# A quarter of the second layer's row maxima taken from half sums and half differences of the keys

## The reference, cut to what matters

```
x_n = (x - mu) * rsqrt(var + eps) * ln_gamma + ln_beta
q, k, v = split(x_n @ W_qkv + b_qkv)                 # 16 heads of 8
scores = einsum('bhqd,bhkd->bhqk', q, k) * SCALE
scores = scores - max(scores, axis=-1)
attn = exp(scores); attn = attn / max(sum(attn), 1e-12)
out = einsum('bhqk,bhkd->bhqd', attn, v) @ W_proj + b_proj
```

## Time and profile before

| what | value |
|---|---|
| median of 3 runs | 3652.12 us (3650.84 to 3652.28) |
| the profiled execution, its own time | 3654.05 us |
| its span in the trace | 3652.2 us |
| TensorE busy | 2988.8 us (82%) |
| VectorE busy | 2628.4 us (72%) |
| ScalarE busy | 2149.4 us (59%) |
| second layer's projection, first store to the end | 909.75 to 958.54 us |
| second layer's attention | 958.54 to about 1672 us |

### The profile page before, as it was taken

One profiled execution on the slowest core, in us unless ns is written; L12 is line 12 of the kernel. 1 busy time (PEld: TensorE's weight loads), 2 busy tenths in 40 slices (PEclk: granted clock), 3 DMA queues, 4 the chain that ended last, 5 costly groups with the idle time before them and its releaser, 6 DMA issues. The chain is left out here.

```text
span 3652.2 us, 51682 instructions
## 1 busy us (share of the span) xinstructions
PE 2988.8 (82%) x18320; PEld 1208.1 (33%) x18320; DVE 2628.4 (72%) x6022; ACT 2149.4 (59%) x2736; POOL 454.0 (12%) x601
## 2 busy tenths in 40 slices
PE   2599998897699999996599999976369998989836
PEld 1133333343222222223355555554332222222214
DVE  4699995476699999984566666641678888888831
ACT  2166666222277777784355545542269989989822
POOL 2000000333100000000000000003231010102023
PEclk9699999998699999998699999987779999999968
DMA  5532220422531211200000000011263222221102
GB/s 201 154 54 46 49 42 2 94 47 54 181 50 35 39 32 30 31 1 4 30 1 1 1 7 1 7 52 43 78 147 55 33 31 30 28 36 23 52 15 81
DMA packets 168110, 173.42 MB, mean 47 GB/s; under 512 B 46648, under 2 KB 126280, under 8 KB 165296
## 3 DMA queue, kind: packets, MB, share of 16 engines
q1 hardware_dynamic: 163760, 162.38, 20.8%
q0 software_dynamic: 4096, 7.78, 0.7%
HBM read 107.71 MB, written 62.26 MB: 47 GB/s over the span
## 5 line engine op out<-in xcount | busy, mean ns | idle before, releaser
L1194 ACT ACTIVATE a_probs<-a_scores 128x1024 f32<-128x1024 f32 (+3 forms) x896 | 791.3, 932 | 374.9 <-PE a_scores L1091 234.2
L1217 DVE TENSOR_REDUCE a_part_max<-a_slot_ps 128x1 f32<-128x512 f32 x1280 | 798.0, 682 | 42.2 <-PE a_slot_ps L1069 40.6
L1069 PE MATMUL a_slot_ps<-a_k_op,a_q_op 48*128 48x512 bf16 (+3 forms) x1792 | 579.7, 380 | 123.1 <-DMA a_mask_wide<-in_mask_wide 32.4
L2214 DVE TENSOR_TENSOR a_probs<-a_logit_ps,a_gate 128x1024 f32<-128x1024 f32 x512 | 602.0, 1218 | 98.0 <-ACT a_gate L2073 96.4
L2078 ACT ACTIVATE a_probs<-a_probs 128x2048 f32<-128x2048 f32 x256 | 488.0, 1906 | 8.6 <-DVE a_probs L2214 8.6
L1091 PE MATMUL a_scores<-a_q_op,a_k_op 51*128 51x512 bf16 (+3 forms) x1792 | 453.2, 362 | 7.1 <-ACT a_probs L1194 6.1
L1111 PE MATMUL a_o_ps<-a_probs,a_v_op 128*32 128x512 f32 (+3 forms) x3584 | 438.1, 561 | 1.2 <-ACT a_o_sb L1181 0.6
L1069 PEld LDWEIGHTS a_slot_ps<-a_k_op,a_q_op 48*128 48x128 bf16 x1792 | 150.3, 94 | 725.0 <-DVE a_part_max L1217 468.2
L1979 PE MATMUL a_logit_ps<-space 96*128 96x512 bf16 x1024 | 303.0, 387 | 72.4 <-DVE a_probs L2214 64.0
L2073 ACT ACTIVATE a_gate<-a_diff_ps 128x1024 f32<-128x1024 f32 x256 | 261.3, 1021 | 54.9 <-PE a_diff_ps L1979 47.3
L1992 PE MATMUL a_o_ps<-a_probs,a_v_op 128*32 128x512 f32 x2048 | 274.6, 608 | 7.0 <-DVE a_o_sb L2207 3.1
(11 more groups left out here) (389 smaller groups left out, 3777.0 us busy)
## 6 DMA issues: line engine op xcount, KB each, us to landing
scratch_v<-p_vpad SPq DMA_DIRECT2D x16, 1024.0 KB, 7.4
a_v_op<-scratch_v SPq DMA_DIRECT2D x32, 512.0 KB, 6.0
e_coef<-coef_dram SPq DMA_DIRECT2D x16, 1024.0 KB, 9.5
a_q_op<-scratch_q SPq DMA_DIRECT2D x384, 32.0 KB
a_k_op<-scratch_k SPq DMA_DIRECT2D x384, 32.0 KB
scratch_q<-p_parts SPq DMA_DIRECT2D x24, 384.0 KB, 4.5
scratch_k<-p_parts SPq DMA_DIRECT2D x24, 384.0 KB, 5.0
space<-scratch_k SPq DMA_DIRECT2D x192, 32.0 KB
```

What stands on the lines that cost most here:

```text
L1069: nc.tensor.matmul(out[:, 0:width], q_op[g][r0:r0 + MAX_ROW, e, qt * P:(qt + 1) * P], k_op[g][r0:r0 + MAX_ROW, e, kh * CH:kh * CH + width] ...
L1194: nc.scalar.activation(probs[gs % NB][:, 2 * e:2 * e + 2, off:CH], scores[e][:, :, off:CH], ACT.Exp, scale=scale).then_inc(probs_done, 1)
L1217: nc.vector.tensor_reduce(part_max[u % 2][:, kh, col:col + 1], slot[:, 0:w], axis=AX.X, op=ALU.max).then_inc(slot_done, 1)
L2214: nc.vector.tensor_tensor(probs[gs % 4][:, m, :, :], logit_ps[m][:], gate[gs % 2][:], op) \
```

## The change

Write k1 for a key of the first half and k2 for the key 512 places behind it. The larger of the two scores q.k1 and q.k2 is q.s + |q.d| with s = (k1 + k2)/2 and d = (k1 - k2)/2. For the odd heads of a pair and the odd row tiles, a quarter of all, the two slots of a row tile now hold q.d (the "difference" slot) and q.s (the "sum" slot). ScalarE takes the absolute value of the difference slot into `sizes` and so releases its bank; VectorE skips that slot, and at the sum slot it adds `sizes` and reduces in one operation (`tensor_tensor_reduce`). The order of eight slots is EIGHT, with three other slots between a difference and its sum. The half sums and half differences of the keys are made in the projection, from W/2 and -W/2, as two more items of every odd chunk. They go to a new scratch and are loaded as `k_halves`.

```diff
-    NB, ITEMS = 4, 2
+    NB = 4
+    items = [(c, kind) for c in range(CHUNKS) for kind in ("qksd" if halves is not None and c % 2 else "qk")]
...
+                    if kind in "qk":
+                        dram = (qs if kind == "q" else ks)[b, :, :, half * CH:(half + 1) * CH]
+                    else:
+                        dram = halves[b, "sd".index(kind)]
...
+                        te.wait_ge(halved, 2)
+                        nc.tensor.matmul(item_ps[n % NB][:], w_half[0][:], xnT[(c - 1) % 4][:], start=True, stop=False)
+                        nc.tensor.matmul(item_ps[n % NB][:], w_half["sd".index(kind)][:], xnT[c % 4][:], start=False, stop=True) \
...
 class NarrowShape:
 
+    EIGHT = ((0, 0, 0), (1, 0, 0), (0, 0, 1), (1, 1, 0), (0, 1, 0), (1, 0, 1), (0, 1, 1), (1, 1, 1))
...
+            self.slots = [(2 * e + jj, qt + odd, kh) for e in range(2) for qt in range(0, KB, 2) for jj, odd, kh in self.EIGHT]
...
+            apart = key[0] == "slot" and self.apart(key[2])
+            count[apart] += 1
+            self.released.append((apart, count[apart]))
...
+            if self.halves is not None:
+                for i in range(2):
+                    src = self.halves[b, i, kp, g * 32:(g + 1) * 32, :].rearrange("(e h r) t -> h r e t", e=2, h=2)
+                    r0 = HALF_ROWS + n * 8
+                    sp.dma_start(self.k_halves[g][r0:r0 + 8, i, :, :], src[1, :, :, :]).then_inc(self.qk_loaded[g], 16)
...
                 if n >= BANKS:
-                    te.wait_ge(slot_done, n - BANKS + 1)
+                    apart, count = shape.released[n - BANKS]
+                    te.wait_ge(size_done if apart else slot_done, count)
...
+                if shape.in_pair(s):
+                    keys = operands.k_halves[g][r0:r0 + MAX_ROW, 1 - kh, e, :]
...
+                    if apart:
+                        act.wait_ge(slot_ready, n + 1)
+                        if count > 2:
+                            act.wait_ge(slot_done, shape.released[shape.place["slot", *pairs[count - 3]]][1])
+                        nc.scalar.activation(sizes[(count - 1) % 2][:], slot_ps[n % BANKS][:], ACT.Abs).then_inc(size_done, 1)
...
+                        slot_sizes(todo[cut[2 * e]:cut[2 * e + 1]])
                         act.wait_ge(scores_ready, gs * 2 + e + 1)
...
+                        slot_sizes(todo[cut[2 * e + 1]:cut[2 * e + 2]])
...
+                if shape.apart(s):
+                    return
                 dve.wait_ge(slot_ready, n + 1)
+                if shape.in_pair(s):
+                    count = pairs.index((u, s)) + 1
+                    dve.wait_ge(size_done, count)
+                    nc.vector.tensor_tensor_reduce(out=slot[:], in0=slot[:], in1=sizes[(count - 1) % 2][:], scale=1.0,
+                                                   scalar=-3e38, op0=ALU.add, op1=ALU.max,
+                                                   accum_out=part_max[u % 2][:, kh, col:col + 1]).then_inc(slot_done, 1)
+                    return
```

More of the change, by code:

```diff
@@ L899, in __init__, with in_pair, apart @@
         self.n = len(self.steps)
-        self.place = {}
+        self.place, self.released = {}, []
+        count = {False: 0, True: 0}
         for key in self.slot_order():
             self.place[key] = len(self.place)
+            apart = key[0] == "slot" and self.apart(key[2])
+            count[apart] += 1
+            self.released.append((apart, count[apart]))
+    def in_pair(self, s):
+        j, qt, kh = self.slots[s]
+        return not self.causal and j % 2 == 1 and qt % 2 == 1
+    def apart(self, s):
+        return self.in_pair(s) and self.slots[s][2] == 0
     def off(self, hq, kb):
@@ L940, with __init__ @@
 class NarrowOperands:
[L943 removed]
+    def __init__(self, nc, ctx, name, shape, qs, ks, vs, halves=None):
         def sb(n, shp, dt=FP32):
@@ L1012, in narrow_attention @@
         block = ctx.enter_context(nc.Block())
-        N_QK, N_MAX = 4 * len(PAIR_PARTS), 6
+        N_QK, N_MAX = operands.loads, 6
+        pairs = [key[1:] for key in shape.place if key[0] == "slot" and shape.in_pair(key[2]) and not shape.apart(key[2])]
         def column_of(j, qt):
@@ L1164, in _ @@
                 out = max_parts[u % 2]
-                pool.wait_ge(slot_done, shape.place["max", u, 0] + 1)
+                pool.wait_ge(slot_done, shape.released[shape.place["max", u, 0]][1])
                 if u >= 2:
@@ L1181, in copy_out, with slot_sizes @@
                 nc.scalar.activation(o_sb[hq][:], o_ps[:], ACT.Copy).then_inc(o_copied, 1)
+            def slot_sizes(todo):
+                for u, s in todo:
+                    n = shape.place["slot", u, s]
+                    apart, count = shape.released[n]
+                    if apart:
[3 more added lines that the diff above has]
+                        nc.scalar.activation(sizes[(count - 1) % 2][:], slot_ps[n % BANKS][:], ACT.Abs).then_inc(size_done, 1)
+            slot_sizes([(0, s) for s in range(NA)])
+            slot_sizes([(1, s) for s in shape.head_start()])
             for u in range(UNITS):
@@ L1185, in _ @@
                     off, gs = shape.off(hq, kb), u * S + n
+                    todo = shape.ahead(u, n)
+                    cut = [len(todo) * p // 4 for p in range(5)]
                     if n == 1 and u > 0:
@@ L1220, in row_maxima @@
             def row_maxima(u):
-                dve.wait_ge(slot_done, shape.place["slot", u, NA - 1] + 1)
+                dve.wait_ge(slot_done, shape.released[shape.place["slot", u, NA - 1]][1])
                 nc.vector.tensor_tensor(row_max[:], part_max[u % 2][:, 0, :], part_max[u % 2][:, 1, :],
```

99 lines of the change are left out of this document (60 added, 39 removed).

## The result

Over seven runs of each on one chip the changed kernel takes 3666.52 us (median, 3663.78 to 3671.10) and the kernel before 3654.36 (3650.84 to 3660.17). The ratio is 1.0034, 95% interval 1.0022 to 1.0046: 12.2 us slower, between 8 and 17. The prediction had +8.4 and 3660.5 us.

What follows compares the result with a forecast made beforehand. The loop was taken as bound by a chain of slot, reduction and bank release, not VectorE's load, and the projection by DMA. Loop 0, head -4.1 and projection +12.5 gave +8.4 us: 3660.5 us, range 3651 to 3676.

Steps and rivals of the forecast that it cites:

- the ring a, its reduction, d, the values, next a: Second layer's attention loop: first slot's matmul, VectorE's reduction, fourth slot in the freed bank, values block; sets the 2.49 us step.
- The loop: 0: Second layer's attention loop: no time change, bounds -1 and +6 us; VectorE loses one reduction in eight and stands idle instead.
- The fits: Loop: other waits fit the step; VectorE by 0.05 us, fourth slot with 0.2 to spare, next exponential at most 0.05 late.
- The head: -4.1: Attention's start, 84 slots, 11 skipped by VectorE: -5 us, plus 0.9 once for the later table load; between -5.8 and -3.6.
- the -5: Attention's start: the gain taken from skipped reductions, before the table load; VectorE alone would give -5.8 us.
- my own reckoning of the banks: Attention's start: with three banks and slower matmuls VectorE goes short some 0.12 us per eight slots, giving -4.5 us.
- The projection: +12.5: DMA-bound stage before attention: eight more items of half sums and differences cost 12.5 us, bounds +8.5 and +15.
- Its two terms: Projection: 9.5 us for 3.35 MB more of stores and loads, 3 us for twelve more small loads on SP's queue.
- The estimate from the Trainium skill (DMA: Bandwidth & Descriptors, Measured): Projection: twelve small loads cost 8 to 11 us if none overlap, against 3.5 counted; the sum would be +13 to +16.
- the occupancy rule of the Trainium skill (Perfetto Trace Analysis, Identifying the Most-Contended Engine): Rival, loop: busy share makes VectorE the bound, so 65 us less, 3595 us; chance 0.08.
- Elsewhere: 0: Rest of the kernel: no cost; a unit's 36 loads instead of 24 take 13 of its 42 us of SP's time.
- The sum: Whole kernel: 0 - 4.1 + 12.5 = +8.4 us, ends at +1.7 and +17.4; predicted median 3660.5 us.

Runs made afterwards that it cites:

- the attention alone: The changed kernel with plain keys in every slot and no halves computed, stored or loaded: 3651.6 us, 0.9991 of the kernel before.
- the packed kernel: The changed kernel with steps of five and three slots, difference first, and only odd heads' halves, packed in one item per odd chunk: 3638.5 us, ratio 0.9932.
- the second experiment: The kernel before with the reductions of a step's second, third and fourth slots halved to 256 of 512 columns: 3642.6 us, ratio 0.9965.
- the two timings: The changed kernel timed twice against the kernel before: 3666.52 us (ratio 1.0034), then again beside other runs, 3666.2 us (1.0030).

## Why the prediction was right, step by step

- *What bounds the loop: the ring a, its reduction, d, the values, next a.* Borne out. Halving a's reduction pays, halving the other three doesn't, and a later d costs.
- *The loop: 0.* The unit is the same to 0.01 us, in the change and in the attention alone. The fits were as tight as written. Of the times counted from a: d at 3.66 came at 2.49 + 1.16 = 3.65 (1302.75 to 1306.40); the sum's bank, free at 3.00, let c load at 3.02 (1305.24 to 1308.26); the absolute value is 0.60 us long, as its nearest row. VectorE's busy time fell by 67.3 of 600 us, where 117 x 0.558 gives 65 for the whole loop, and its idle time stands where it was put, ahead of the a behind a difference.
- *The head: -4.1.* It was -3.0, by the first unit's maxima (64 of the 84 slots) and by the first exponential alike. The table load is as forecast: the first exponential stands 49.36 us behind the stage's start, 2.94 less than the 52.30 of the earlier trace rows, so with the group's 0.39 x 10.5 = 4.1 us the load costs some 1.1 (forecast 0.9). What was off is the -5: my own reckoning of the banks gave -4.5 and I went beyond it, and the shortfall is 0.16 us a group (4.39 less 4.23), not 0.12.
- *The projection: +12.5.* It was +12.4. Its two terms: 9.5 for bytes, by the packed kernel 3.15 x 3.15 = 9.9, and 3 for twelve loads, measured 3.0 by the times and 4.1 by the traces. Together that is 12.9 to 14.0, so the parts taken alone come to 0.5 to 1.6 us more than the whole, and the agreement to 0.1 us is closer than its terms, which is luck. The rate was 308 GB/s over the stage and not near 320 up to its end; it fell to 116 beside the last small loads. The engines were done 24.8 us before the stage's end, not 24.9; nothing hangs on that.
- The estimate from the Trainium skill (DMA: Bandwidth & Descriptors, Measured), 8 to 11 us for the twelve loads if none overlap, isn't borne out: they cost 0.25 to 0.34 us each. That table is for transfers over 128 partitions issued from GpSimd, and these are loads of 8 partitions that SP issues one behind the other. By the occupancy rule of the Trainium skill (Perfetto Trace Analysis, Identifying the Most-Contended Engine) VectorE was the engine to relieve; the trace of the second experiment disagrees, 369 us of work instead of some 530 in the same time.
- *Elsewhere: 0.* The halves' loads in the loop delay nothing, as the unit shows.
- The sum was +8.4, the traces have +9.7 (of which the head's 1.1 is most), the two timings +12.2 and +10.2. The 2.5 us by which the first timing exceeds the traces stand in no row; its interval starts at 8. The 6 us between 3660.5 and 3666.5 are the 3.8 from +8.4 to +12.2, and 2.2 by which the kernel before itself was above its first three runs.

What stays open: why the projection's two terms, measured one by one, come to more than the whole, and how the head's shortfall of 0.16 us a group splits between bank and matmul.

## What to carry to other kernels

Before you take work from an engine, ask which of its instructions is waited for. Here VectorE was 99% busy, and halving three quarters of its reductions gained nothing in the loop, while halving the fourth paid in full. Where few buffers go round between the engines, as the three banks do here, it is the order of the slots and who frees each buffer that set the step. The time that the change freed on VectorE was there, and became 33 us only when the slot that ScalarE frees was put where two releases would otherwise stand in a row. And what this change stored in a stage bound by DMA was paid in full, so only the halves that are read should be stored.

## What the runs showed of the hardware

- Loads of 16 KB issued one behind the other on SP's queue cost 0.25 to 0.34 us each in a stage bound by DMA, about the time of their issue (0.30 us long, 0.34 to 0.35 apart); stores of 384 KB cost 1.24 us each (4.95/4), which is their bytes at 317 GB/s.
- VectorE at 99% busy by the profile wasn't the bound: its instructions overlap by some 0.08 us (0.68 long, 0.598 apart), so an instruction that starts 0.1 us late leaves almost no idle time to see.
- In the head, at a granted clock of 0.50, a slot's reduction started 0.65 us behind its weight load (957.65 to 958.30, 962.49 to 963.14), where in the loop, at 1.00, it was 0.42 (1305.24 to 1305.66). With 48 of 64 reductions halved the slots still took 0.43 us each.
- ScalarE's absolute value of a 128x512 bank is 0.60 us long and VectorE's reduction of it 0.68, so the next matmul into the bank could load 1.07 us behind the last one's load instead of 1.17.
